# Scores behind the output product, the softmax's maximum ahead of the gate, the exponential ahead of the copies of y

## The reference

```python
q = l2norm(q) * qs; k = l2norm(k) * ksc
q = q * cos * scale + rotate_half(q) * sin * scale
sim = einsum('bhwie,bhwje->bhwij', bq, bk2) * 8.0     # windows of 32, 64 keys
attn = softmax(where(mask, -max, sim))
out = einsum('bhwij,bhwje->bhwie', attn, bv2)
x = out @ Wo + x
hg = layernorm(x) @ W1 + b1; a, gate = split(hg)
x = a * gelu(gate) @ W2 + b2 + x
```

## Time and profile before

| | |
|---|---|
| median of 3 runs | 4592.19 us |
| the profiled execution | 4594.7 us |
| its span, first to last instruction | 4592.9 us |
| TensorE busy (PE) | 4344.7 us, 95% |
| VectorE busy (DVE) | 3911.2 us, 85% |
| ScalarE busy (ACT) | 2982.6 us, 65% |
| GpSimd busy (POOL) | 2810.1 us, 61% |
| mean granted TensorE clock | 0.991 |

### The profile page before, as it was taken

How to read it: one execution, slowest core, us unless ns; L and a number is a source line. 1 busy time by engine, 2 the same in 40 slices (tenths; PEclk the granted TensorE clock), 3 DMA queues, 4 the chain that set the end, 5 groups by cost and what they waited for, 6 DMA issues and landing times. The chain is left out here.

```text
span 4592.9 us, 102400 instructions
## 1 busy us (share of the span) xinstructions
PE 4344.7 (95%) x36584; PEld 3036.2 (66%) x36584; DVE 3911.2 (85%) x5311; ACT 2982.6 (65%) x4227; POOL 2810.1 (61%) x4591
## 2 busy tenths in 40 slices
PE   5999999999899999999999999999999999999997
PEld 3555455555467777777777777777777777777775
DVE  6888788888688988898888899888988889989994
ACT  4666666666456676666666667666667667667663
POOL 3555555555466666666665666666666666666672
PEclk9999999999999999999999999999999999999998
DMA  1000000000110101101011111111011110111010
GB/s 53 3 6 5 3 5 3 5 3 3 33 43 22 31 24 34 48 25 30 26 40 40 27 28 32 45 27 33 24 33 47 27 31 25 28 52 27 26 30 14
DMA packets 256467, 119.39 MB, mean 26 GB/s; under 512 B 118336, under 2 KB 251456, under 8 KB 255168
## 3 DMA queue, kind: packets, MB, share of 16 engines
q1 hardware_dynamic: 256192, 115.87, 9.2%
HBM read 86.31 MB, written 16.91 MB: 22 GB/s over the span
## 5 line engine op out<-in xcount | busy, mean ns | idle before, releaser
L580 POOL TENSOR_TENSOR pn<-es,rden 128x1024 f32<-128x1024 f32 x192 | 366.6, 1909 | 779.1 <-DVE rden L915 779.1
L564 POOL TENSOR_TENSOR t<-t,ardn 128x1024 f32<-128x1024 f32 x256 | 485.1, 1895 | 304.1 <-DVE ardn L800 303.8
L674 ACT ACTIVATE y<-ps 128x1024 f32<-128x1024 f32 x384 | 372.2, 1021 | 349.6 <-PE ps L1116 349.6
L665 ACT ACTIVATE t<-ps,anm,srn 128x512 f32<-128x512 f32 x512 | 392.9, 771 | 271.1 <-DVE anm L809 271.1
L584 POOL TENSOR_TENSOR t<-t 128x1024 f32<-128x1024 f32 x192 | 454.7, 2368 | 85.1 <-DVE t L867 85.1
L867 DVE TENSOR_TENSOR t<-ps,tabl 128x512 f32<-128x512 f32 x768 | 490.1, 679 | 0.0
L865 DVE TENSOR_TENSOR t<-ps,tabl 128x1024 f32<-128x1024 f32 x384 | 466.5, 1215 | 16.8 <-ACT sq L690 13.3
L954 DVE TENSOR_REDUCE mx<-ps 128x16 f32<-128x1024 f32 x192 | 235.1, 1225 | 259.0 <-PE ps L1238 255.4
L586 POOL TENSOR_TENSOR t<-t 128x1024 f32<-128x1024 f32 x192 | 452.9, 2359 | 2.7 <-DVE t L867 2.7
L964 DVE TENSOR_TENSOR qn<-t,rn 128x2048 f32<-128x2048 f32 x192 | 437.9, 2281 | 5.8 <-POOL rn L389 5.8
L925 DVE TENSOR_REDUCE ss<-sq 128x32 f32<-128x2048 f32 x192 | 436.4, 2273 | 0.0
(11 more groups left out here) (136 smaller groups left out, 9329.5 us busy)
## 6 DMA issues: line engine op xcount, KB each, us to landing
xw<-tokens_dram SPq DMA_DIRECT2D x768, 64.0 KB, 1.9
tokens_dram<-x SPq DMA_DIRECT2D x96, 128.0 KB
xs<-tokens_dram SPq DMA_DIRECT2D x192, 64.0 KB, 1.9
xsh<-x SPq DMA_DIRECT2D x48, 128.0 KB
xsh<-x SPq DMA_DIRECT2D x48, 127.0 KB
wm<-in_l_wqk SPq DMA_DIRECT2D x3, 1024.0 KB, 4.9
wv<-in_l_wv SPq DMA_DIRECT2D x6, 512.0 KB, 3.9
wo<-in_l_wo SPq DMA_DIRECT2D x6, 512.0 KB, 5.4
```

The source lines that it names most:

```text
L564: nc.gpsimd.tensor_tensor(eA[:, v], eA[:, v], ardn[:, v].unsqueeze(2).to_broadcast([P, 2, SEQ]), ALU.mult).then_inc(a_pn, 1)
L665: e = act.activation(eA[:, j, h], bank(j % 2 * 2 + h), ACT.Exp, bias=anm[:, j, h:h + 1], scale=srn[:, a % 2, j, h:h + 1], accum_out=aden[: ...
```

## The change

Three moves, the same work. TensorE makes mask and scores directly behind the output product (and behind the fold and the FFN's bias sums, in the turns that have them), ahead of the FFN's piece and of the transposes of pn and xs. VectorE takes maximum and subtraction directly behind the output sum, ahead of the gate, the FFN's sum and the bias. ScalarE makes the exponential behind xT, ahead of the two copies of y, and the dummy exponential goes, with its tile. The waits go along with their instructions, unchanged.

```diff
 ScalarE
-                if s.has(2) and (s.ffn(2) if c == 0 else c >= 2 and s.ffn(1)):
-                    act.activation(edge[:], zero[0:1, 0:1], ACT.Exp)
+                if s.has(2):
+                    act.wait_ge(l_sub, t + 3)
+                    act.activation(es[:], es[:], ACT.Exp, scale=QK_SCALE).then_inc(l_e, 1)
                 if s.has(1):
                     act.wait_ge(l_y, t + 2)
                     past(act, l_o, t + 1)
                     copy_y(0, pool2).then_inc(l_y0sb, 1)
                     copy_y(1, pool0).then_inc(l_y1sb, 1)
-                if s.has(2):
-                    act.wait_ge(l_sub, t + 3)
-                    act.activation(es[:], es[:], ACT.Exp, scale=QK_SCALE).then_inc(l_e, 1)
 VectorE
                     nc.vector.tensor_tensor(xb, xb, ps_o, ALU.add).then_inc(l_x, 1)
+                if s.has(2):
+                    dve.wait_ge(l_s, t + 3)
+                    nc.vector.tensor_reduce(mx[:], heads(pool1, H), X, ALU.max).then_inc(l_mx, 1)
+                    dve.wait_ge(l_mx, t + 3)
+                    past(dve, l_p, t + 2)
+                    nc.vector.tensor_tensor(heads(es[:], H), heads(pool1, H),
+                                            mx[:].unsqueeze(2).to_broadcast([P, H, KEYS]), ALU.subtract).then_inc(l_sub, 1)
                 if c == 0 and s.ffn(2):
                     gate(s.f2, 2)
...
                 if c >= 2 and s.ffn(1):
                     gate(s.f1, c - 2)
-                if s.has(2):
...
 TensorE
                 if s.turn_of(1, 1):
                     pe.wait_ge(l_qT, t + 3)
                     ffn_bias(s.l)
+                if s.has(2):
+                    u = (c + 2) % NU
+                    if s.has(3):
+                        pe.wait_ge(l_rk, t + 4)
+                        pe.wait_ge(l_sqk, t + 4)
+                    else:
+                        past(pe, l_sub, t + 2)
+                    pe.wait_ge(l_qT, t + 3)
+                    pe.wait_ge(l_kT, t + 3)
+                    for i in range(2):
+                        half = slice(i * KEYS, (i + 1) * KEYS)
+                        nc.tensor.matmul(pool1[:, i * 512:(i + 1) * 512], msel[half, 0 if u == 0 else 1], ...)
+                    for a in range(PAIRS):
+                        for w in range(NW):
+                            m = nc.tensor.matmul(pool1[w * WIN:(w + 1) * WIN, a * 2 * KEYS:(a + 1) * 2 * KEYS], ...)
+                    m.then_inc(l_s, 1)
                 if s.has(3):
                     pe.wait_ge(l_rq, t + 4)
                     pe.wait_ge(l_sqq, t + 4)
...
                     nc.tensor.transpose(ps_x[:, 0:P], xs[:, c], ident).then_inc(l_xt, 1)
-                if s.has(2):
...
                 if s.has(1):
                     u = (c + 1) % NU
                     pe.wait_ge(l_pT, t + 2)
```

More of the change, by code:

```diff
@@ L117, in build @@
         zero = sb("zero", [WIN, DIM])
-        edge = sb("edge", [1, 1])
         xw = sb("xw", [P, NU, NW, DIM])
@@ L1186, in turn @@
                     ffn_bias(s.l)
+                if s.has(2):
[9 more added lines that the diff above has]
+                        half = slice(i * KEYS, (i + 1) * KEYS)
+                        nc.tensor.matmul(pool1[:, i * 512:(i + 1) * 512], msel[half, 0 if u == 0 else 1],
+                                         mask[half].rearrange("p h k -> p (h k)"), start=True, stop=False, skip_group_check=True)
+                    for a in range(PAIRS):
+                        for w in range(NW):
+                            key0 = u * P + w * WIN
+                            m = nc.tensor.matmul(pool1[w * WIN:(w + 1) * WIN, a * 2 * KEYS:(a + 1) * 2 * KEYS],
+                                                 qT[:, a, w * WIN:(w + 1) * WIN], kpad[:, 2 * a:2 * a + 2, key0:key0 + KEYS],
+                                                 start=False, stop=True, skip_group_check=True)
+                    m.then_inc(l_s, 1)
                 if s.has(3):
```

## The result

The changed kernel takes 4932.4 us, the median of 4 runs from 4929.73 to 4932.73, against 4592.6. The ratio is 1.0739, with an interval from 1.0720 to 1.0758: 340 us slower. The profiled execution takes 4929.73, its span is 4927.9 against 4592.9, 335 us more. The forecast was 4928.

A forecast was written before the change was run, and what follows sets the result against it. TensorE's queue was taken to bound the kernel. The profiled 4594.7 us plus 293 for holes and 43 for the clock gave 4931, and 4928 us for the median, 2.5 us lower; range 4866 to 4975.

The forecast's parts named there:

- The hole: TensorE idle ahead of the window products, waiting for copy xT: 1.39 us in 142 turns, 197.4 us.
- The bound of plus or minus 0.20: Hole of 1.19 us without the hand-over from xT, 1.59 with a second one: -38 or +38 us over 190 turns.
- The turns with the long hole: Turns c = 0, copies late behind the gelu's table load: TensorE stands 2.44 us, 2.20 more in 42 turns, 92.4 us.
- The wait of the scores for the rotation of k: Scores behind the output product wait for VectorE's rotate of k: taken as 0, up to 58 us if it fails.
- the four turns with the tables: Turns where the next layer's tables are scaled and VectorE is late: extra wait of the scores taken as 0.
- VectorE's and ScalarE's moves: Maximum and subtraction ahead of the gate, exponential ahead of the copies of y without the dummy: cost 0 each.
- The clock: TensorE at half clock after long holes of turns c = 0: 28 times 1.53 us, 43 us.
- the two thirds: Share of the 42 long holes assumed to be followed by half clock: 28 turns; none is -43 us, all +21.
- Rival 1: Holes appear ahead of the window products but TensorE's clock holds: 4885 us, chance 0.22.
- Rival 2: Half clock follows the 1.39 us holes too, adding 145 us: 5073 us, chance 0.07 with anything else above 4985.
- the turns with the bias sums: Six turns where the transpose of xs waits for new bias sums: hole of 0.6 us each, 3.6 us.
- Rivals 3 and 4: 3: VectorE's chain is the path, 4565 us, chance 0.03; 4: TensorE takes projections first, filling the hole, 4592 us, 0.02.

The follow-up runs named there:

- The filler: The full change plus three useless matmuls in the hole ahead of the window products, in turns c = 0 with a gelu: 4888.3 us.

## Why the prediction came out

The lengths of turns below are from start to start of the output products, and the sums are over the 191 turns from the first output product of the layers to the last.

**The hole.** Right in place and count, and in size by the profile: 272.6 us in 189 waits, where near 270 in some 190 were forecast. The turn c = 2 grew by 1.43 us instead of 1.39, by two errors that cancel, which is luck. xT hands over in 0.05 us (3378.83 to 3378.88) and not in 0.20, so the hole costs 0.15 less. In exchange two groups have a longer share of the queue by about 0.1 each: 3.74 us from output product to scores instead of 3.65, and 1.82 instead of 1.72 for the FFN's piece. The bound of plus or minus 0.20 held this. The turns c = 1 and c = 3 grew by 1.39 and 1.55, and all regular turns together (139) by 194 us, 1.40 each, where 142 times 1.39 = 197 was forecast.

**The turns with the long hole.** One without half clock lasts 19.0 us, and 16.6 before: 2.38 longer and not 2.20. The small losses of the regrouping come on top here too. Times 42 this is 8 us too little. The prediction called all 42 of them turns c = 0; 38 are, and four are turns c = 2 that load the gelu's table just as late.

**The wait of the scores for the rotation of k.** Costed at 0 and 0. In the regular turns that is what the trace shows. In the four turns with the tables there was a gain that I missed: they lasted 21.9, 22.0, 22.0 and 20.4 us before, with the wait of 2.45 us and three half clocks in them, and 19.15 after, so they are 9.7 us shorter. The sum had each of them 1.39 longer, which makes it 15 us too much. I had set the earlier start of the chain against its later link and called it even. The chain started earlier by more. Whose move this is has two answers: with TensorE's move alone these turns last 22.1 to 23.7 us, with VectorE's alone 19.1 and with ScalarE's alone 18.0. The last two are the length of the other turns c = 1 of those runs, so either move takes the wait out by itself.

**VectorE's and ScalarE's moves.** Cost 0, as forecast, but only together with TensorE's. Alone they cost 227 and 21 us. In the full change the copies of y start 2.22 us behind the window products' start (forecast 2.0 to 2.2) and nobody waits for them. The Trainium skill ("ScalarE: Activation LUTs", What ACT_TABLE_LOAD costs) gives a table switch a drain beside its load, and the trace decides against it: in the earlier trace rows and in the 3378.84 row the next instruction starts within 0.02 us of the load's end, and in the latter the load itself starts 0.01 us behind the copy of xT.

**The clock.** 43 us were forecast, at 28 of 42 turns. Counted in the trace, 31 of the 42 holes have a stretch at half clock that begins between 0.4 us before the hole's end and 1.4 us behind it. With one such a turn grew by 4.00 us on average, without by 2.38: 1.62 each (1.53 forecast), 50 us in all. That the two thirds, chosen after four cases, were near the mark is partly luck: with qT in halves it is 18 of 42 for holes of the same size. The filler took out 27 of the 31 and brought 44 us. Rival 1 (the clock holds) would have come out near 4882 by this count, and it had 4885. (The prediction's sentence that the page's rule gives the time of the second rival means this one, the first.) Rival 2 (the small holes lower the clock) fell with the full change itself, where none of the small holes is followed by a half clock, and with the scores behind the FFN's piece: 0.993. The Trainium skill ("TensorE: Matmul & The Clock Gate", Why this matters for your kernels) warns only of idle gaps longer than these. The measurement decides: a gap of 2.3 us cost the clock three times in four here.

**The sum.** Regular turns 194 us (197 forecast), long holes 100 (92), the turns with the bias sums 4 (4), the clock 50 (43), the turns with the tables -10 (0, and their 1.39 each stands in the 197): 338 us in these turns, 335 in the span, and 336 forecast. The mechanism and its main terms are right. That the total is right to 2 us is luck: two terms were 7 to 8 us too small and one 15 us too large. Rivals 3 and 4 are refuted by the result.

## What to carry to other kernels

When a queue is full, ask of each group what it hides, not only what it waits for. The scores waited for nothing between the transposes and the window products, and were the cover for two copies; whatever moves them must leave 1.4 us of other work there. A hole near 2.4 us on TensorE can cost more than itself (here 1.6 us more in 31 of 42 cases), and even useless matmuls in it paid. A regular wait of 0.4 us that recurs in each turn is worth a split copy: it gave 2 percent where the larger reordering lost 7. And when moves are tested alone, look at the rare turns too: here four of 191 turns held 10 to 15 us.

## What was not expected

- The hand-over from xT to the window products varies: 0.05 us in the turn c = 2, 0.19 to 0.20 in c = 0.
- None of the 141 holes for xT of 1.2 to 1.4 us in the full change, nor of the 189 with the scores behind the FFN's piece, is followed by a half clock. Of the 42 holes of 2.3 to 2.4 us, 31 are. With qT in halves the same 42 holes are followed by one only 18 times.
- ScalarE's move alone and the split copy of qT alone also took out the 2.45 us wait of the turns with the tables (the latter all but 0.3 us of it), which neither was aimed at.
- Moving a group in TensorE's queue costs about 0.1 us at its new neighbour, though no work and no wait is added.
